# Cross-attention over a long context on one core: two batches a step, each with all its keys on 64 TensorE columns

## The chip, the core and the metric

One core of a Trainium2 chip runs the whole program in one launch. The metric is the device time of an execution in microseconds (us). The kernel before took 1009.78, 1009.5 and 1008.39 us in three runs; their median, 1009.5 us, is what the change is compared with.

## The reference, cut to what matters

The block is layer norm, self-attention, cross-attention, a two-layer feed-forward part, a gated recurrent layer and a mixture of eight experts. The change is in the cross-attention. It has 16 batches of 64 query rows and 1601 context rows, all 512 wide:

```python
def cross_attn(x, context, Wq, Wk, Wv):
    Q = x @ Wq
    K, V = (context @ Wk, context @ Wv)
    energy = jnp.einsum('bqd,bkd->bqk', Q, K)
    Sk = energy.shape[-1]
    lengths = jnp.sum(energy[:, 0] != 0, axis=-1)
    kidx = jnp.arange(Sk)
    pad = kidx[None, None, :] >= lengths[:, None, None]
    energy = jnp.where(pad, NEG_INF, energy)
    score = jax.nn.softmax(energy / np.sqrt(DK), axis=-1)
    return jnp.einsum('bqk,bkd->bqd', score, V)
z = cross_attn(x, context, Wq2, Wk2, Wv2)
x = layer_norm(x + z, ln2_g, ln2_b)
z = jax.nn.relu(x @ fc1_w + fc1_b)
z = z @ fc2_w + fc2_b
```

The kernel folds the weights: the queries are multiplied by Wq times the transposed Wk, scores are taken against the raw context, and Wv is applied to the attention's output. So the context is wanted in two layouts, both in HBM and both loaded: `ctxT`, with the 512 features on the partitions (for the scores), and `ctx`, with keys on the partitions (for the weighted sums, called values below).

## The kernel before, in words

Every engine has its own program, written out by hand in program order, and the programs meet in semaphores. TensorE does the matmuls (weight loads are a row of their own in the profile, PEld), VectorE (DVE) and ScalarE (ACT) evacuate PSUM, GpSimd (POOL) makes the low parts of weights, and SyncE (SP) issues all loads of this stage, in order, each behind the waits that stand ahead of it.

Cross-attention runs in 17 rounds, one batch a round, and each round finishes the batch before. TensorE's array is used in two halves of 64 columns: the two halves take the same 64 queries and different keys of one batch, the wide one 833 keys and the narrow one 768, and `WIDE` alternates which half is wide. A TensorE round n is:

- `scores(n)` (L621): two pieces of up to 512 columns, four chunks of features, two halves.
- `transpose_probabilities(n-1)` (L631): 7 transposes, the last of 65 columns.
- `transpose_output(n-2)` (L663): 4 transposes of the attention's output.
- a filling, by the tables `LATE` (part of the queries of later batches, L598) or `VALUE` (`value_rows(i)`, the product with Wv of token tile i, 12 matmuls of split fp32 at L486).
- `exchange(n)` (L670, L673): maxima and sums of the two halves are swapped between them and the keys counted.
- `values(n-1)` (L650, 12 matmuls, and L654, the 65 last keys, on one half alone).

VectorE counts the non-zero scores (`count_keys`, L1469), builds the mask and takes the row maximum (`shift`, L1490 and L1495), combines the halves' factors (`normaliser`), adds the two halves' outputs (`output_sum`, L1525), makes the low part of the output (`output_low`, L1533) and, after a `value_rows(i)`, adds it to x and normalises (`second_norm(i)`: L1538, L1315, L1317, L1320, POOL's L1935, L1332, L1336). ScalarE does the exponential (L1102) and scaled copies. `decay_start`, `decay_term` and `decay_end` are a chain of small VectorE operations for the recurrent layer (`lac`), spread over the rounds.

`VALUE` puts tiles 0 to 5 into rounds 9 to 14 and tile 6 into round 16, ahead of the last values. Tile 7 follows the loop. There TensorE does the transposes `t2` of the normalised rows (L493, in groups of four tiles' quarters), the last output's transposes, `value_rows(7)`, and then the first half of fc1 (L486 on `f1u`).

The context is held in two whole-batch buffers for each layout (`cT`, `nat`). SP loads `ctxT` of batch n+1 once the scores of n-1 are done with the buffer (`e_done`), and `ctx` of batch n once the values of n-2 are (`pv_done`):

```python
def load_columns(n):
    load(cT[n % 2], a["ctxT"][n].rearrange("p (c k) -> p c k", c=DC), ct_in[n % 2])
```

At the start, both layouts of two batches are loaded before any score is taken. The weight units of fc1 (`f1u`) are loaded after the scores of the last batch; ScalarE makes their high part and POOL their low part (L1958).

## Time and profile before

| | |
|---|---|
| three runs | 1008.39 to 1009.78 us, median 1009.5 |
| profiled execution | 1006.8 us, of which the span is 1005.1 |
| TensorE busy (PE) | 985.9 us, 98% of the span |
| VectorE, ScalarE, GpSimd busy | 614.8, 393.7, 215.9 us |
| cross-attention, first scores to first fc1 matmul | 112.55 to 370.46 us of the span |
| chain that ended last | PE 85%, DVE 7%, DMA 6% |
| loaded from HBM | 190 MB, mostly context |

The profile is of one execution, 2.7 us shorter than the median of the runs. Times in rows are microseconds from the start of the span. A group of matmuls in a timeline is one row with a count; the bracket behind a row says how long its engine had been idle and what released it. A KB of the profile's DMA issues is 1024 bytes.

### The profile page before, as it was taken

The numbers are of one execution on the slowest core, as the hardware profiler recorded it, in microseconds if no ns is written. First come the engines' busy times: TensorE is split into PE (matmuls) and PEld (weight loads), VectorE is DVE, ScalarE is ACT, GpSimd is POOL, SyncE is SP. The second block draws the span as 40 slices with busy tenths as digits, with TensorE's granted clock in tenths as the row PEclk, the third lists the DMA queues.
The fourth block names the chain that finished last, engine by engine and source line by source line (L and its number), as shares of the span: only waits on it lengthen the run. The fifth ranks groups of instructions, "written<-read, shape, count | busy, mean of one in ns | idle before, by whom it ended". The sixth has DMA issues, their size and how long they took to land.

```text
span 1005.1 us, 14411 instructions
## 1 busy us (share of the span) xinstructions
PE 985.9 (98%) x5412; PEld 777.0 (77%) x5412; DVE 614.8 (61%) x1142; ACT 393.7 (39%) x631; POOL 215.9 (21%) x202
## 2 busy tenths in 40 slices
PE   7999999999999999999999999899999999999998
PEld 4886444445454468878888887899999999999997
DVE  6368443344655565896466668577665666656666
ACT  3332211222111143355667542444544444445441
POOL 2053400002000036454422124720000000000051
PEclk9999999999999999999999999999999999999999
DMA  9809599999999922033311100885764756645543
GB/s 295 317 1 381 241 361 417 409 414 397 415 396 408 388 94 74 1 92 108 110 42 38 32 1 7 277 283 156 217 188 151 206 159 196 189 155 183 152 150 133
DMA packets 45959, 206.91 MB, mean 206 GB/s; under 512 B 5760, under 2 KB 16256, under 8 KB 41680
## 3 DMA queue, kind: packets, MB, share of 16 engines
q1 hardware_dynamic: 40256, 187.95, 52.6%
q0 software_dynamic: 5648, 18.22, 5.4%
q8 instruction: 34, 0.56, 0.2%
q14 instruction: 21, 0.17, 0.0%
HBM read 190.04 MB, written 16.12 MB: 205 GB/s over the span
## 4 chain that ended last, share of the span: by engine, by line
PE 85%; DVE 7%; DMA 6%; issue 1%; ACT 0%; SPq 0%; POOL 0%; DVEq 0%; ACTq 0%
PE ps L486 59%; PE ps L621 7%; PE ps L650 7%; DMA big<-in_ctxT 3%; DMA big<-in_ctx 2%; DVE stats L1315 2%; PE ps L480 2%; PE ps L598 1%; PE ps L951 1%; PE ps L856 1%; PE ps L978 1%; PE ps L654 1%; PE ps L631 1%; PE ps L493 1%; DVE hr L1324 1%; PE ps L532 1%
## 5 line engine op out<-in xcount | busy, mean ns | idle before, releaser
L486 PE MATMUL ps<-x,w 128*128 128x320 f32 x1536 | 235.6, 309 | 0.0
L486 PEld LDWEIGHTS ps<-x,w 128*128 128x128 f32 x1536 | 228.0, 188 | 0.4
L1839 DVE TENSOR_TENSOR w<-big,w 128x1536 fp32r<-128x1536 f32 x64 | 112.1, 1753 | 78.3 <-ACT w L1249 78.3
L486 PE MATMUL ps<-hsplit,w 128*128 128x320 f32 x672 | 107.7, 309 | 0.0
L1249 ACT CAST w<-big 128x1536 fp32r<-128x1536 f32 x64 | 94.2, 1475 | 29.2 <-PE ps L486 27.0
L486 PEld LDWEIGHTS ps<-hsplit,w 128*128 128x128 f32 x672 | 100.8, 188 | 0.1
L486 PE MATMUL ps<-xcT,u 128*128 128x512 f32 x432 | 98.2, 389 | 0.0
L621 PE MATMUL ps<-big 128*64 128x512 f32 (+2 forms) x512 | 95.9, 500 | 0.7 <-DVE s_stat L1495 0.6
L486 PEld LDWEIGHTS ps<-xcT,u 128*128 128x128 f32 x432 | 81.0, 188 | 17.0 <-DVE xcT L1627 0.2
L650 PE MATMUL ps<-big 128*64 128x512 f32 x384 | 86.4, 597 | 1.7 <-DMA big<-in_ctx 1.5
L621 PEld LDWEIGHTS ps<-big 128*64 128x64 f32 x512 | 44.2, 136 | 51.0 <-issue 39.1
L1271 ACT CAST hsplit<-big 128x320 fp32r<-128x320 f32 x64 | 29.4, 460 | 137.9 <-DVE big L1869 137.9
L1958 POOL TENSOR_TENSOR u<-big,u 128x512 fp32r<-128x512 f32 (+1 forms) x40 | 59.4, 1493 | 103.5 <-ACT u L1088 103.5
L2043 POOL DMA_DIRECT2D ys<-big x28 | 16.8, 603 | 276.3 <-DVE big L1861 275.3
L1935 POOL TENSOR_TENSOR rstd<-veps,consts 128x1 f32<-128x1 f32 x48 | 34.0, 709 | 182.2 <-DVE veps L1320 181.9
L486 PE MATMUL ps<-hT,u 128*128 128x512 f32 x288 | 66.0, 390 | 0.8 <-DVE big L1616 0.7
L486 PEld LDWEIGHTS ps<-hT,u 128*128 128x128 f32 x288 | 53.9, 188 | 12.6 <-issue 0.9
L650 PEld LDWEIGHTS ps<-big 128*64 128x64 f32 x384 | 26.1, 137 | 46.8 <-issue 44.8
L1474 DVE COPY big<-ps 128x512 f32<-128x512 f32 x16 | 11.1, 691 | 77.3 <-PE ps L631 77.3
L1020 ACT COPY big<-ps 128x512 f32<-128x512 f32 (+1 forms) x48 | 24.5, 543 | 75.1 <-PE ps L486 47.3
L1873 DVE TENSOR_TENSOR hsplit<-big,hsplit 128x320 fp32r<-128x320 f32 (+1 forms) x72 | 32.0, 454 | 33.7 <-ACT hsplit L1271 33.7
L1102 ACT ACTIVATE big<-big,s_work 128x833 f32<-128x833 f32 x16 | 15.8, 991 | 59.8 <-DVE s_work L1498 59.8
(336 smaller groups left out, 1544.6 us busy)
## 6 DMA issues: line engine op xcount, KB each, us to landing
big<-in_ctxT SPq DMA_DIRECT2D x16, 3202.0 KB, 19.3
big<-in_ctx SPq DMA_DIRECT2D x16, 3072.0 KB
big<-in_w_units SPq DMA_DIRECT2D x64, 768.0 KB, 4.4
big<-in_dense_units SPq DMA_DIRECT2D x41, 256.0 KB, 2.7
xs<-big POOLq DMA_DIRECT2D x1, 5120.0 KB, 17.4
big<-in_gate_units SPq DMA_DIRECT2D x12, 384.0 KB, 3.0
hr<-xs SPq DMA_DIRECT2D x28, 160.0 KB, 5.8
ys<-big POOLq DMA_DIRECT2D x28, 160.0 KB, 5.6
```

The lines of the kernel that those rows point to most:

```text
L480: mm = nc.tensor.matmul(bank(*g)[:, 0:cols], lhsT, rhs, start=(k == 0), stop=(k == len(pairs) - 1))
L486: mm = nc.tensor.matmul(dst, lhs[x], rhs[w], start=start and x + w == 0, stop=stop and x == 1)
L621: mm = nc.tensor.matmul(ps[half * S:half * S + S, 2 + piece, 0:w], qT[:, d, n * S:(n + 1) * S], cT[n % 2][:, d, col:col + w], start=(d == ...
L650: mm = nc.tensor.matmul(ps[half * S:half * S + S, 6, :], pts[:, t, half * S:half * S + S], nat[j][:, narrow * KH + t, :], start=(t == 0), ...
L1020: signals_evacuated(nc.scalar.copy(dst, src_bank), *g)
L1249: nc.scalar.copy(wsplit[f % RING][0][:], wraw[f % RING]).then_inc(w_high, 1)
L1271: nc.scalar.copy(hsplit[f % 2][:, 0:SLOTS], hid[f % 2]).then_inc(hid_high, 1)
L1315: V.bn_stats(stats[:, i, :], src).then_inc(ln_stats, 1)
L1839: V.tensor_tensor(wsplit[f % RING][1][:], wraw[f % RING], wsplit[f % RING][0][:].bitcast(F32), ALU.subtract).then_inc(w_low, 1)
L1873: V.tensor_tensor(h[:, to:to + hi - lo], hid[f % 2][:, lo:hi], h[:, lo:hi].bitcast(F32), ALU.subtract).then_inc(hid_low, 1)
L1935: G.tensor_tensor(rstd[:, i:i + 1], veps[:, i:i + 1], consts[:, 0:1], ALU.pow).then_inc(ln_rstd[L], 1)
L1958: G.tensor_tensor(low[:, 0:w], unit_raw(u)[:, 0:w], high[:, 0:w].bitcast(F32), ALU.subtract).then_inc(u_low, 1)
```

## The change

A step p now takes two batches, 2p and 2p+1, each with all 1601 keys on its own 64 columns of TensorE. There are nine steps instead of 17 rounds.

- `scores(p)` (new L634) has three pieces of 512 keys and one of 65, four chunks, two halves, in four PSUM banks. `transpose_probabilities(p)` (L656) has 12 transposes into three banks; the thirteenth, of the last 65 keys (L674), stands beside the count's matmul (L677). The swap of maxima and sums, the factors and `output_sum` are gone. `values(p)` has 24 matmuls (L691) and 2 for the last keys (L698). `transpose_output` comes once a pair, and `output_low(p)` (L1522) reads PSUM and writes 512 columns.
- VectorE's passes over the scores are 1601 columns wide instead of 833, once a pair.
- `VALUE` gives a step up to two tiles, one ahead of the values and one behind; step 8 has tile 6 behind the last values. `late_queries(p)` comes whole in steps 0 to 3.
- The context goes through five ring slots of two buffers, 8 KB a partition each (1 MB a load). Columns and rows share the slots, which are filled in the order of use: three slots of columns of pair p+1, three of rows of pair p. A slot is loaded again when its piece has been used (`piece_used`). The last 65 columns and rows have two small buffers each. `ctxT` is packed in pieces in HBM. fc1's units are loaded after piece 45 of 48 was used.

```diff
-PIECES = ((0, 512, 512), (512, KA - 512, KH * P - 512))
-WIDE = [n // 2 % 2 for n in range(B)]
-LATE = {1: (0, 0, 2), 2: (0, 2, 4), 3: (1, 0, 2), 4: (1, 2, 4), 5: (2, 0, 4), 6: (3, 0, 2), 7: (3, 2, 4)}
-VALUE = {9: 0, 10: 1, 11: 2, 12: 3, 13: 4, 14: 5, 16: 6}
+PAIRS = B // 2
+PIECES = KT // 4
+RINGS = 5
+VALUE = {5: (0, 1), 6: (2, 3), 7: (4, 5), 8: (None, 6)}
...
-            def load_context(n):
-                j = n % 2
-                load(nat[j][:, 0:KT, :], a["ctx"][n, 0:KT * P, :].rearrange("(p k) d -> p k d", k=KT), nat_in[j])
-                load(nat[j][0:TAIL, KT, :], a["ctx"][n, KT * P:SK, :], nat_in[j])
-
-            def load_columns(n):
-                load(cT[n % 2], a["ctxT"][n].rearrange("p (c k) -> p c k", c=DC), ct_in[n % 2])
+            def load_pieces(rows, p):
+                for piece in range(PIECES):
+                    g = loads[0]
+                    loads[0] += 1
...
+                    if g >= RINGS:
+                        sp.wait_ge(piece_used, g - RINGS + 1)
+                    for half in range(2):
+                        n, to = 2 * p + half, context_at[g % RINGS][half]
+                        if rows:
+                            keys = a["ctx"][n, 0:KT * P, :].rearrange("(p k) d -> p k d", k=KT)
+                            load(to, keys[:, 4 * piece:4 * piece + 4, :], context_in[g % RINGS])
+                        else:
+                            load(to, a["ctxT"][n * PIECES + piece].rearrange("p (c k) -> p c k", c=DC), context_in[g % RINGS])
...
             load_columns(0)
-            load_context(0)
-
-            for i in range(NT):
-                wait_filled(sp, "z", i)
-            load_columns(1)
-            load_context(1)
-            sp.wait_ge(e_done, 1)
-            load_columns(2)
-            for n in range(2, B):
-                if n + 1 < B:
-                    sp.wait_ge(e_done, n)
-                    load_columns(n + 1)
-                if n == 8:
+            for p in range(1, PAIRS):
+                load_columns(p)
+                if p == 5:
                     sp.wait_ge(late_q, DC)
                     for k in range(DC):
                         load(z2_raw[k], a["dense_units"][k], u_in[k])
-                sp.wait_ge(pv_done, n - 1)
-                load_context(n)
-            sp.wait_ge(e_done, B)
+                load_rows_of(p - 1)
+            load_rows_of(PAIRS - 1)
+            sp.wait_ge(piece_used, 2 * PAIRS * PIECES - PIECES)
...
+            def scores(p):
...
+                for piece in range(PIECES + 1):
...
                     for d in range(DC):
...
-                        for half in (WIDE[n], 1 - WIDE[n]):
-                            narrow = half != WIDE[n]
-                            col, w = narrow * KA + lo, widths[narrow]
+                        for half in range(2):
+                            n, w = 2 * p + half, 512 if piece < PIECES else TAIL
                             mm = nc.tensor.matmul(ps[half * S:half * S + S, 2 + piece, 0:w], qT[:, d, n * S:(n + 1) * S],
-                                                  cT[n % 2][:, d, col:col + w], start=(d == 0), stop=(d == DC - 1))
-                mm.then_inc(e_done, 1)
+                                                  columns_in[half][:, d, :], start=(d == 0), stop=(d == DC - 1))
+                    mm.then_inc(piece_used if piece < PIECES else e_done, 1)
...
+            for p in range(PAIRS + 1):
+                if p < PAIRS:
+                    scores(p)
+                if p == 0:
+                    late_transposes(4, NT - 1)
+                    tail_and_count(0)
+                    late_transposes(NT - 1, NT)
+                    late_queries(0)
+                    continue
+                transpose_probabilities(p - 1)
+                if p >= 2:
+                    transpose_output(p - 2)
+                tail_and_count(p)
+                if p < PAIRS // 2:
+                    late_queries(p)
+                ahead, behind = VALUE.get(p, (None, None))
+                if ahead is not None:
+                    value_rows(ahead, 3 * p)
+                values(p - 1)
+                if behind is not None:
+                    value_rows(behind, 3 * p)
...
             split_transposes("t2", 0)
             split_transposes("t2", 1)
-            transpose_output(B - 1)
+            transpose_output(PAIRS - 1)
             split_transposes("t2", 2)
-            pe.wait_ge(o_evac, 2 * B - 1)
+            pe.wait_ge(o_evac, PAIRS)
             split_transposes("t2", 3)
-            value_rows(NT - 1)
+            value_rows(NT - 1, 3 * PAIRS)
...
+            for p in range(PAIRS + 1):
+                if p < PAIRS:
+                    count_keys(p)
+                tail_and_count(p)
+                if p < PAIRS:
+                    shift(p)
+                if p:
+                    normaliser(p - 1)
+                if p >= 2:
+                    output_low(p - 2)
+                for i in VALUE.get(p, ()):
+                    if i is not None:
+                        second_norm(i)
...
+                if p == 8:
+                    decay_end()
+            output_low(PAIRS - 1)
```


How the instructions stand on three engines, where it matters:

SP's loads at the start, before (`in_ctxT` is the context with features on the partitions, `in_ctx` that with keys):

```order
L368 DMA big<-in_ctxT 128x6404
L368 DMA big<-in_ctx 128x6144
L368 DMA big<-in_ctx 65x512
L368 DMA big<-in_ctxT 128x6404
L368 DMA big<-in_ctx 128x6144
L368 DMA big<-in_ctx 65x512
L368 DMA big<-in_ctxT 128x6404 x2
```

and with the change:

```order
L363 DMA big<-in_ctxT 128x2048 x6
L363 DMA big<-in_ctx_tails 128x520
L363 DMA big<-in_ctxT 128x2048 x6
L363 DMA big<-in_ctx_tails 128x520
L363 DMA big<-in_ctx 128x2048 x6
L363 DMA big<-in_ctx 65x512 x2
```

One batch's columns and rows were two large loads and a small one; now three slots of columns, six loads of 2048 elements a partition, come for a pair, with one small load for the last columns.

TensorE's last round of the loop and what follows it, before (`z2u` are parts of Wv, `oT` the transposed output):

```order
L631 MATMUL ps<-ident,big 128x128 x6
L631 MATMUL ps<-ident,big 65x128
L663 MATMUL ps<-ident,big 128x128 x4
L486 MATMUL ps<-z2u0high,oT_high 128x512
...
L486 MATMUL ps<-z2u3high,oT_low_74 128x512
L670 MATMUL ps<-s_stat,swap 128x2
L650 MATMUL ps<-big 64x512 x12
L654 MATMUL ps<-big 64x512
L493 MATMUL ps<-ident,hr 128x128 x8
L663 MATMUL ps<-ident,big 128x128 x4
L493 MATMUL ps<-ident,hr 128x128 x8
L486 MATMUL ps<-z2u0high,oT_high 128x512
```

and with the change, from the last scores (its L493 is the line that was L486):

```order
L634 MATMUL ps<-big 64x512 x24
L634 MATMUL ps<-big 64x65 x8
L656 MATMUL ps<-ident,big 128x128 x12
L667 MATMUL ps<-ident,big 128x128 x4
L674 MATMUL ps<-ident,big 65x128
L677 MATMUL ps<-s_cnt,first_rows 128x1
L493 MATMUL ps<-z2u0high,oT_high 128x512
...
L493 MATMUL ps<-z2u3high,oT_low_74 128x512
L691 MATMUL ps<-big 64x512 x24
L698 MATMUL ps<-big 64x512 x2
L493 MATMUL ps<-z2u0high,oT_high 128x512
```

`value_rows(6)` stood ahead of the last values and the `t2` transposes right behind them; now value rows 5 (the first `z2u` rows) stand ahead of the last values, and value rows 6 between those and the transposes.

VectorE's end of the stage, before (the normaliser's last operation has gone ahead; `hr` is the second norm of tile 6, `oT_low_75` the last output's low part, `hT` the first operand of fc1):

```order
L1533 TENSOR_TENSOR oT_low_75<-oh_rk,oT_high 128x4x64
L1538 TENSOR_TENSOR hr<-hr,ps 128x512
L1315 BN_STATS stats<-hr 128x6
L1317 BN_AGGR mv<-stats 128x2
L1320 TENSOR_SCALAR veps<-mv 128x1
L1332 SCALAR_TENSOR_TENSOR hr<-hr,mv,lnw 128x512
L1336 SCALAR_TENSOR_TENSOR hr<-hr,rstd,lnw 128x512
L1525 TENSOR_REDUCE oh_rk<-ps 128x256
L1533 TENSOR_TENSOR oT_low_75<-oh_rk,oT_high 128x4x64
L1580 TENSOR_TENSOR hT_115<-ps,hT_114 128x4x128 x4
```

and with the change:

```order
L1527 TENSOR_TENSOR hr<-hr,ps 128x512
L1335 BN_STATS stats<-hr 128x6
L1337 BN_AGGR mv<-stats 128x2
L1340 TENSOR_SCALAR veps<-mv 128x1
L1352 SCALAR_TENSOR_TENSOR hr<-hr,mv,lnw 128x512
L1356 SCALAR_TENSOR_TENSOR hr<-hr,rstd,lnw 128x512
L1469 TENSOR_TENSOR lac<-lac 128x6
L1470 TENSOR_SCALAR lac<-fbase 128x6
L1472 SCALAR_TENSOR_TENSOR lac<-lac 128x6
L1473 SCALAR_TENSOR_TENSOR lac<-lac 128x6
L1522 TENSOR_TENSOR oT_low_75<-ps,oT_high 128x512
L1566 TENSOR_TENSOR hT_115<-ps,hT_114 128x4x128 x4
```

The last output's low part was behind the second norm of tile 6 too; now four operations of `decay_end` (`lac`) stand between, and the second norm waits for value rows that come after the last values.

## Rows read from the trace of the kernel before

**Rows 1.** Page, DMA issues: tensors, queue, count, KB each, us to landing.

```profile
big<-in_ctxT SPq DMA_DIRECT2D x16, 3202.0 KB, 19.3
big<-in_ctx SPq DMA_DIRECT2D x16, 3072.0 KB
```

**Rows 2.** Windows: stretch, us, busy PE, PEld, DVE, ACT, POOL (count), PEclk, DMA, GB/s.

```profile
76.00:140.00 64.00, 60.96 (x262) 32.97 (x262) 38.56 (x77) 14.44 (x38) 19.36 (x16) 1.00 0.79 317
80.00:108.00 28.00, 26.74 (x97) 16.65 (x96) 26.96 (x46) 5.68 (x11) 15.39 (x14) 1.00 1.01 423
140.00:180.00 40.00, 40.00 (x215) 19.43 (x213) 17.60 (x58) 9.15 (x23) 0.00 (x0) 1.00 1.01 415
140.00:340.00 200.00, 199.77 (x1045) 99.14 (x1043) 101.11 (x309) 40.73 (x100) 8.51 (x10) 1.00 1.01 407
256.60:338.20 81.60, 81.50 (x426) 42.62 (x425) 46.39 (x138) 14.00 (x35) 2.74 (x5) 1.00 1.00 402
631.00:636.00 5.00, 5.00 (x41) 4.99 (x41) 1.55 (x11) 1.75 (x4) 2.99 (x4) 1.00 0.99 415
643.00:644.00 1.00, 1.00 (x5) 1.00 (x5) 1.00 (x1) 0.02 (x1) 0.69 (x2) 0.50 0.26 102
```

**Rows 3.** Timeline, TensorE's weight loads: start, us, engine, line, operation, [idle before <-releaser].

```profile
256.60 0.20 PEld L621 LDWEIGHTS ps<-big 128*64 128x64 f32 x4 [0.78 <-DMA big<-in_ctxT]
...
338.22 0.20 PEld L621 LDWEIGHTS ps<-big 128*64 128x64 f32 x4 [0.74 <-DMA big<-in_ctxT]
...
346.90 0.20 PEld L650 LDWEIGHTS ps<-big 128*64 128x64 f32 x4 [1.75 <-DMA big<-in_ctx]
```

**Rows 4.** Chain of waits, 280 to 306: start, us, what (one round).

```profile
289.50 5.81 PE ps L621 x30
...
296.22 0.44 PE ps L663 x4
296.66 2.75 PE ps L486 x12
...
299.74 5.30 PE ps L650 x24
305.04 0.85 PE ps L654 x2
```

**Rows 5.** Timeline, first scores, 112 to 123.

```profile
112.55 5.81 PE L621 MATMUL ps<-big 128*64 128x512 f32 x32
...
118.42 1.02 DVE L1469 TENSOR_SCALAR_CACHE_REDUCE big<-ps 128x833 f32<-128x833 f32 x1 [4.87 <-PE ps L621]
...
122.32 1.08 PE L621 MATMUL ps<-big 128*64 128x512 f32 x4 [0.62 <-DVE s_stat L1495]
```

**Rows 6.** Timeline, end of cross-attention, 340 to 371.

```profile
340.93 0.16 DVE L1449 TENSOR_TENSOR lac<-lac 128x6 f32<-128x6 f32 x1
...
360.22 0.68 DVE L1538 TENSOR_TENSOR hr<-hr,ps 128x512 f32<-128x512 f32 x1
363.36 1.02 PE L654 MATMUL ps<-big 65*64 65x512 f32 x2
363.48 0.75 DVE L1336 SCALAR_TENSOR_TENSOR hr<-hr,rstd,lnw 128x512 f32<-128x512 f32 x1
...
367.57 0.50 PE L486 MATMUL ps<-z2u0high,oT_high 128*128 128x512 f32 x1 [0.24 <-DVE oT_low L1533]
...
370.46 0.86 PE L486 MATMUL ps<-hT,f1u 128*128 128x512 f32 x3
```

**Rows 7.** Timeline, last normalisation before the fc1 activations, 370 to 377.

```profile
370.66 0.69 DVE L1538 TENSOR_TENSOR hr<-hr,ps 128x512 f32<-128x512 f32 x1 [0.76 <-PE ps L486]
...
373.08 3.00 POOL L1958 TENSOR_TENSOR f2u<-big,f2u 128x512 fp32r<-128x512 f32 x2
...
374.96 1.67 DVE L1336 SCALAR_TENSOR_TENSOR hr<-hr,rstd,lnw 128x512 f32<-128x512 f32 x1
```

**Rows 8.** Timeline, TensorE after a long wait in the last stage.

```profile
642.45 0.54 PE L856 MATMUL ps<-pick,row4high 128*128 128x320 f32 x1 [2.84 <-DVE pick L1764]
```

More of the change, by code:

```diff
@@ L610, in scores @@
+            used = [0]
+            def scores(p):
+                if p:
+                    pe.wait_ge(shifted, p)
+                else:
                     for c in range(DC - 1):
                         wait_evacuated(pe, "q", c)
-                for piece, (lo, *widths) in enumerate(PIECES):
-                    if piece and n % 2 == 0:
-                        pe.wait_ge(pad_cleared, n // 2 + 1)
+                if p == PAIRS // 2:
+                    pe.wait_ge(late_q_out, DC)
+                for piece in range(PIECES + 1):
+                    if piece < PIECES:
+                        g = used[0]
+                        used[0] += 1
+                        pe.wait_ge(context_in[g % RINGS], 32 * (g // RINGS + 1))
+                        columns_in = context_at[g % RINGS]
+                    else:
+                        pe.wait_ge(column_tail_in[p % 2], 16 * (p // 2 + 1))
+                        columns_in = column_tails[p % 2]
@@ L615, in scores @@
                     for d in range(DC):
-                        if n == 0 and d == DC - 1:
+                        if p == 0 and piece == 0 and d == DC - 1:
                             wait_evacuated(pe, "q", DC - 1)
-                        for half in (WIDE[n], 1 - WIDE[n]):
-                            narrow = half != WIDE[n]
-                            col, w = narrow * KA + lo, widths[narrow]
+                        for half in range(2):
+                            n, w = 2 * p + half, 512 if piece < PIECES else TAIL
@@ L637, in values @@
-            def values(n, lo, hi):
-                j = n % 2
-                if lo == 0:
-                    pe.wait_ge(nat_in[j], 32 * (n // 2 + 1))
-                    pe.wait_ge(pt_evac[0], n + 1)
-                    if n:
-                        pe.wait_ge(o_copied, n)
-                else:
-                    pe.wait_ge(pt_evac[1], 2 * n + 2)
-                for t in range(lo, hi):
-                    for half in (WIDE[n], 1 - WIDE[n]):
-                        narrow = half != WIDE[n]
-                        mm = nc.tensor.matmul(ps[half * S:half * S + S, 6, :], pts[:, t, half * S:half * S + S],
-                                              nat[j][:, narrow * KH + t, :], start=(t == 0), stop=(narrow and t == KH - 1))
-                if hi == KH:
-                    w = slice(WIDE[n] * S, WIDE[n] * S + S)
-                    mm = nc.tensor.matmul(ps[w, 6, :], pts[0:TAIL, KH, w], nat[j][0:TAIL, KT, :], start=False, stop=True)
-                    mm.then_inc(pv_done, 1)
@@ L1134, in _ @@
                     nc.scalar.copy(fbias[:], lnw[:, 6, :]).then_inc(fb_high, 1)
+                if p == 4:
+                    for u in range(DC):
+                        unit_high(u)
             def transposed_high(name, i):
@@ L1153, in _ @@
             transposed_high("t2", 1)
-            output_out(B - 1)
+            output_out(PAIRS - 1)
             unit_high(5)
@@ L1541, in second_norm @@
                 norm_gain(2, i, hr[:, i, :], lnw[:, 3, :])
-            for n in range(B + 1):
-                if n:
-                    probabilities_out(n - 1)
-                if n < B:
-                    count_keys(n)
-                if n >= 2:
-                    output_sum(n - 2)
-                exchanged(n)
-                if n < B:
-                    shift(n)
-                if n:
-                    normaliser(n - 1)
-                if n >= 2:
-                    output_low(n - 2)
-                if n in VALUE:
-                    second_norm(VALUE[n])
-                if n == 6:
-                    decay_start()
-                if 7 <= n < 7 + ATANH_TERMS - 2:
-                    decay_term(ATANH_TERMS + 5 - n)
-                if n == 5 + ATANH_TERMS:
-                    decay_end()
-                if n == 4:
+            for p in range(PAIRS + 1):
+                if p < PAIRS:
+                    count_keys(p)
+                tail_and_count(p)
+                if p < PAIRS:
+                    shift(p)
+                if p:
+                    normaliser(p - 1)
+                if p >= 2:
+                    output_low(p - 2)
+                for i in VALUE.get(p, ()):
+                    if i is not None:
+                        second_norm(i)
+                if p == 2:
                     dve.wait_ge(fb_high, 1)
@@ L1569, in _ @@
                     V.tensor_tensor(fbias[S:P, :], lnw[S:P, 6, :], fbias[S:P, :].bitcast(F32), ALU.subtract).then_inc(fb_low, 1)
-            output_sum(B - 1)
-            output_low(B - 1)
+                if p == 3:
+                    decay_start()
+                if 4 <= p < 8:
+                    for k in range(ATANH_TERMS - 2 - 2 * (p - 4), max(ATANH_TERMS - 4 - 2 * (p - 4), 0), -1):
+                        decay_term(k)
+                if p == 8:
+                    decay_end()
+            output_low(PAIRS - 1)
             dve.wait_ge(lnw_in, 16)
```

360 lines of the change are left out of this document (161 added, 199 removed).

## The prediction, made before the changed kernel was run

> **What bounds the kernel now.** I read first the page's DMA issues, then windows over cross-attention, then TensorE's waits in it, then its end. A batch brings 3202 KB of `ctxT`, 3072 KB of `ctx` and 130 KB of last rows (65 rows of 2 KB, from the code), 6404 KB or 6.56 MB [rows 1]. From 140 to 340 us the DMA engines are busy all the time at 407 GB/s, and TensorE is busy all the time too [rows 2]. The stage is bound by both, and the timeline of weight loads says how closely: at 256.60 and, five batches later, at 338.22 the scores wait 0.78 and 0.74 us for their `ctxT` [rows 3]; I counted four more such waits between. Five batches in 81.62 us are 16.32 us a batch and 402 GB/s, as the window of that stretch shows. So the load stream sets the pace, and TensorE's round, with value rows, fills it: 5.81 us of scores, 0.44 of output transposes, 2.75 of value rows, 5.30 and 0.85 of values, and some smaller pieces [rows 4].
>
> At the end the stream runs out before TensorE does. The rows of batch 14 come at 346.90 [rows 3]; those of batch 15, 3202 KB, are the last of the context and come 8.2 us later at 402 GB/s, at 355.1. The last values end at 363.36 + 1.02 = 364.4, and fc1 starts at 370.46, 6.1 us behind them [rows 6]. From there on the program is unchanged, so I forecast the start of fc1 and carry its shift to the end.
>
> **The change part by part.**
>
> *TensorE's work in the loop.* A pair's values are 24 + 2 matmuls in both halves: twice 5.30, and one 0.85 for the last keys in place of two. A 512-column piece of scores is 5.81 x 512/833 = 3.6 us; three and the 65 last columns make 11.2 in place of 11.6. Output transposes fall from 0.88 to 0.44 a pair, and the swaps go [rows 4]. That is about 2 us a pair, 16 in all. But a pair with two value rows then takes about 30 us, while its 13.1 MB at 402 GB/s take 32.6. TensorE waits for pieces instead. I cost this saving at nothing; the load stream covers it, and the bytes are the same.
>
> *VectorE and ScalarE.* A pass of 833 columns takes 1.02 us [rows 5]; 1601 columns are 1.96 by proportion, once a pair instead of twice. Busy 101 of 200 us [rows 2], VectorE has room; at the start alone it is waited for (next step).
>
> *The start of the stream.* Before, two batches, 13.1 MB, are loaded ahead, and by 140 us 64 x 0.317 = 20.3 MB have come [rows 2]. The ring holds 5 slots of 2.10 MB and 0.27 MB of last columns, 10.75 MB. At 423 GB/s [rows 2] it is full by about 103, and the stream stands until the first piece is used: scores start at 112.55 [rows 5], plus 3.6 for a piece is 116.1. Before, 20.3 - 13.1 = 7.2 MB came between the issue behind the first scores (118.4) and 140, 17.7 us of stream at 407, so 3.9 us were lost to latency and to the wait for the second scores. With pieces freed every 3.6 us I take 2.4 us of it: from 118.5, 21.5 us at the 415 GB/s of the first window behind 140 [rows 2] are 8.9 MB, in all 19.65. That is 0.65 MB or 1.5 us behind. Bounds: 0.5 (no more than 1.4 us lost) and 3.0 (all 3.9). The second scores wait for the first's VectorE passes: before from 118.4 to 122.32 [rows 5], now 2.5 us more and scores that end 5 us later; they start near 130. TensorE has late transposes and queries there, and the ring is full, so only those 1.5 us count.
>
> *The pace of the stream.* Loads become 1 MB with 8 KB a partition instead of 3.2 MB with 25 KB. No row shows this size. The nearest is the expert weights, 768 KB loads with 6 KB a partition back to back: 415 GB/s [rows 2]. The stream itself went at 415 early and 402 late, 407 on the mean. I take no change, with 1% to either side, 2.2 us on some 217 us of stream. A rule of the Trainium skill speaks against the change here: "DMA: Bandwidth & Descriptors", section "Bandwidth", gives 1 MB transfers 78% of the peak and 16 MB ones 97%. Scaled so from 407 the stream would fall to some 330 GB/s, an estimate from that page, and the sum would be about +55 us. By that rule the 768 KB loads could not have gone at 415 [rows 2]; the trace disagrees, and I give it 2 in 100, within rival C.
>
> *The end of the values.* The last piece lands at 355.1 + 1.5 = 356.6. It has four of twelve key tiles of each batch: 5.30 x 4/6 = 3.5 us, and the last keys 0.85 [rows 4]: 361.0, 3.4 us earlier than before. Here the change gains, since before TensorE still had two batches' leftovers when the stream ended.
>
> *From the last values to fc1.* This is new work in series. Before, `value_rows(6)` came ahead of the last values, and `second_norm(6)` ran beside them, from 360.22 to 363.48 + 0.75 [rows 6]. Now TensorE starts `value_rows(6)` behind them, 2.75 us. The second norm follows: 4.0 us alone [rows 6], 6.0 us from 370.66 to 374.96 + 1.67 where two POOL passes stand beside it [rows 7]. Behind it in VectorE's order come `decay_end`, four operations of 0.16 [rows 6], and only then the last `output_low`, about 0.68 for 512 columns. TensorE's next transposes wait for that: 0.44, then `value_rows(7)` 2.75 and about 0.25 to start each [rows 4, 6]. The last output's own transposes, ready by then, are off this path. The sum is 2.75 + 4.0 + 0.65 + 0.68 + 0.44 + 2.75 + 0.5 = 11.8 us, or 13.8 with POOL's passes beside the norm. POOL's passes come here one by one with ScalarE's casts between, so I take the middle, 12.8.
>
> *The clock.* In that stretch TensorE has 2 us of transposes and an idle time of about 5 us. In the last stage, after an idle time of 2.84 us, its granted clock falls to 0.50, which is 1.2 of 2.4 GHz [rows 2, 8]. The transposes and value rows behind the wait, 3.2 us, cost between nothing and 3.2 us more at that clock; half of it, 1.6, is taken, since the clock came back within a few us in that stage.
>
> **Sum.** 361.0 + 12.8 + 1.6 = 375.4 for the start of fc1, against 370.46: +4.9 us. The profiled execution's 1006.8 us becomes 1011.7; it stands 2.7 below the median of the runs, so the median of 1009.5 becomes **1014.4**. The bounds together are 1.0 to 1.6 us each for start, tail and clock: its own range is 1010.8 to 1018.5.
>
> **The rivals.** A difference below 0.2%, 2 us, is about what a measurement here can't tell from no change.
>
> *A, faster: the stream runs faster in pieces.* The first stretch went at 423 GB/s [rows 2], and 415 is seen for 6 KB a partition. TensorE's 30 us a pair leave room to 437. Each 1% is worth 2.2 us, and since the forecast is +4.9, it takes 3.2%, 420 GB/s, to be faster by 2 us; at 425 it is -9.6, so 1004.8. Against it: the stream's share was full before too, so there is no idle time between loads to win.
>
> *B, about the same: the new tail costs less.* No POOL pass beside the norm (-1.0), no fall of the clock (-1.6), and 0.5% of pace (-1.1) leave +1.2, 1010.7. For it: clock and contention are only seen elsewhere.
>
> *C, much slower: TensorE's clock falls inside the loop.* TensorE now waits in small portions: 3.6 us of piece, then up to 1.8 until the next lands. At half clock a pair's 30 us would become up to 60, more than the 32.6 of its loads; every 2.6 us spent at half clock beyond that slack goes to the end. If a third of the last three pairs ran so, 3 x (40 - 32.6) = 22 us. In this trace waits of 0.7 to 1.75 us left the clock at 1.00 [rows 2, 3], and only the 2.84 did not. The Trainium skill, "TensorE: Matmul & The Clock Gate", section "HAM oscillation — how this bites in real kernels", has kernels where each wait for a slice makes the next start at the low clock; by these rows it would not here, outside the tail. So 1036. A slower pace belongs here too: 395 GB/s, 3% below the mean of 407, is +6.6 on the forecast, 1021.
>
> That the change doesn't do what it says I give nothing: the order of the instructions shows pieces, pairs and tables moved as described.
>
> **How the numbers follow.** Forecast 0.50 (slower), A 0.15 (faster), B 0.20 (the same), C 0.15 (slower). So faster 0.15, same 0.20, slower 0.65. The range 1006.5 to 1020 holds the forecast's own, B, and the near part of A and C; it leaves out about one in ten at either end.
>
> **What the next profile would show.** Right: DMA share full from about 119 to 357 but for gaps near 105 to 118, 402 to 415 GB/s; TensorE waiting for `ctxT` and `ctx` pieces in most of the loop at clock 1.00; the last values ending near 361; then value rows 6, a wait of some 5 us for the last `output_low`, clock 0.5 behind it, fc1 at about 375. Wrong: a stream above 420 GB/s or below 398 in the same stretch; granted clock below 1 inside the loop; fc1 before 372.5 or after 379.

## The result, and the profile after

The changed kernel took 1020.1 us (median of four runs, 1019.28 to 1021.72) against 1009.0 of the kernel before in the same comparison: a ratio of 1.0112, 95% interval 1.0096 to 1.0128, so 11.1 us slower. The direction was forecast, the size was not: +4.9 had been worked out, and 1020.1 lies just above the range's end of 1020. The profiled execution took 1020.73 us with a span of 1019.0, 13.9 more than the span before. fc1 starts at 384.44, 13.98 us later than the 370.46 of [rows 6]. (The two profiled executions lie 2.8 us further apart than the medians: the one before is 2.2 us below 1009.0, the one after 0.6 above 1020.1.) So the whole loss is ahead of fc1, and the two parts of it can be read apart at the end of the last values: 368.1 (forecast 361.0) and 16.3 us from there to fc1 (forecast 14.4).

The page of the changed kernel: the span, TensorE, the chain by engine, and the two large kinds of loads.

```profile
span 1019.0 us, 14013 instructions
PE 977.5 (96%) x5324; PEld 755.8 (74%) x5324; DVE 568.9 (56%) x933; ACT 385.7 (38%) x575; POOL 216.4 (21%) x202
PE 80%; DMA 11%; DVE 8%; issue 1%; SPq 0%; ACT 0%; POOL 0%; DVEq 0%; ACTq 0%
big<-in_ctxT SPq DMA_DIRECT2D x48, 1024.0 KB, 17.2
big<-in_ctx SPq DMA_DIRECT2D x48, 1024.0 KB, 18.1
```

TensorE is 8.4 us less busy and the span is longer: the saved work became waits for loads. Windows over the stage (columns as in [rows 2]):

```profile
76.00:140.00 64.00, 61.36 (x254) 31.16 (x255) 35.27 (x57) 13.39 (x33) 19.36 (x16) 1.00 0.73 295
132.00:134.00 2.00, 2.00 (x12) 0.67 (x10) 0.00 (x0) 1.36 (x2) 0.00 (x0) 1.00 0.79 328
134.00:136.00 2.00, 2.00 (x12) 0.72 (x10) 0.00 (x0) 0.00 (x0) 0.00 (x0) 1.00 0.39 57
136.00:138.00 2.00, 2.00 (x12) 0.61 (x10) 0.00 (x0) 0.00 (x0) 0.00 (x0) 1.00 0.75 283
140.00:340.00 200.00, 183.62 (x943) 76.89 (x941) 58.59 (x134) 34.06 (x54) 7.17 (x8) 0.99 1.01 401
206.00:208.00 2.00, 2.00 (x12) 0.61 (x10) 0.00 (x0) 0.44 (x2) 0.00 (x0) 1.00 1.09 293
208.00:210.00 2.00, 2.00 (x12) 0.71 (x10) 0.00 (x0) 0.00 (x0) 0.00 (x0) 1.00 1.04 267
212.00:214.00 2.00, 2.00 (x12) 0.62 (x10) 0.00 (x0) 0.00 (x0) 0.00 (x0) 1.00 1.02 426
244.00:246.00 2.00, 2.00 (x8) 0.73 (x6) 0.00 (x0) 0.00 (x0) 0.00 (x0) 0.50 0.99 410
340.00:356.00 16.00, 14.86 (x75) 7.05 (x73) 4.39 (x10) 2.96 (x7) 0.92 (x2) 1.00 1.01 367
380.00:382.00 2.00, 2.00 (x7) 1.66 (x6) 1.85 (x3) 1.42 (x3) 0.24 (x1) 0.50 0.14 53
```

By 140 us 64 x 0.295 = 18.9 MB have come, against 20.3 before [rows 2]. The stream stands twice: once until the first piece is used, and again at 132 to 138, when the ring is full once more and the first columns of pair 1 are not yet used. From 140 to 340 it moves 401 GB/s with the DMA engines always busy. That mean hides two speeds: about 420 in most windows of 2 us (their median is 418), and dips of some 4 us, one a pair, here 293 and 267, where the two small loads of last rows of a pair (65 partitions, 2 KB each) pass; run 5 leaves them out, and the dips go. In the dips the DMA share is 1.04 to 1.09: the engines don't stand, they move less. The kernel before has such dips too, down to 298 in a window of 2 us. TensorE's waits for pieces, its last values, POOL's passes, TensorE's long wait at the end and its first matmul of fc1, from the timeline:

```profile
220.70 0.20 PEld L634 LDWEIGHTS ps<-big 128*64 128x64 f32 x4 [2.10 <-DMA big<-in_ctxT]
...
242.34 5.35 PE L691 MATMUL ps<-big 128*64 128x512 f32 x16 [2.42 <-DMA big<-in_ctx]
...
363.59 0.20 PEld L691 LDWEIGHTS ps<-big 128*64 128x64 f32 x4 [1.72 <-DMA big<-in_ctx]
...
367.08 1.03 PE L698 MATMUL ps<-big 65*64 65x512 f32 x4
...
373.55 4.60 POOL L1944 TENSOR_TENSOR f1u<-big,f1u 128x512 fp32r<-128x512 f32 x3
...
379.43 1.11 PE L500 MATMUL ps<-ident,hr 128*128 128x128 f32 x4 [6.58 <-DVE oT_low L1522]
...
384.44 5.84 PE L493 MATMUL ps<-hT,f1u 128*128 128x512 f32 x25
```

Its first wait for a piece is at 215.83 (0.32 us), the first long one at 220.70. From the first on it waits for 16 of 27 pieces, and the last piece comes at 363.59, where 356.6 was forecast. Behind it, the chain of waits:

```profile
363.59 3.65 PE ps L691 x16
367.25 0.86 PE ps L698 x4
368.11 3.01 PE ps L493 x12
...
371.14 0.70 DVE hr L1527
...
373.62 1.76 DVE hr L1352
...
375.40 1.63 DVE hr L1356
377.03 1.15 DVE lac L1469
...
378.68 0.70 DVE oT_low L1522
...
379.43 1.11 PE ps L500 x4
380.54 5.66 PE ps L493 x19
```

This is the series that was forecast: value rows 6, the second norm of tile 6, the decay chain, the last low part, the transposes, value rows 7. The norm takes 5.9 us, with POOL's passes beside its two long ones (1.76 and 1.63 against 0.75 in [rows 6]), and the first small operation 1.15.

### The profile page after: what moved, and what is told of

The parts are those of the page before. It is cut to its first block, busy times and chain, and to the rows that moved or that the text cites. A ratio compares the mean times of both kernels' runs of the same rounds, so it can differ in the third digit from the quotient of the medians.

```text
span 1019.0 us, 14013 instructions
## 1 busy us (share of the span) xinstructions
PE 977.5 (96%) x5324; PEld 755.8 (74%) x5324; DVE 568.9 (56%) x933; ACT 385.7 (38%) x575; POOL 216.4 (21%) x202
## 4 chain that ended last, share of the span: by engine, by line
PE 80%; DMA 11%; DVE 8%; issue 1%; SPq 0%; ACT 0%; POOL 0%; DVEq 0%; ACTq 0%
PE ps L493 58%; DMA big<-in_ctxT 8%; PE ps L634 6%; PE ps L691 4%; DMA big<-in_ctx 2%; DVE stats L1335 2%; PE ps L487 1%; PE ps L606 1%; PE ps L974 1%; PE ps L879 1%; PE ps L1001 1%; PE ps L656 1%; PE ps L500 1%; DVE hr L1352 1%; DVE hr L1344 1%; PE ps L539 1%
## 5 line engine op out<-in xcount | busy, mean ns | idle before, releaser
L493 PE MATMUL ps<-x,w 128*128 128x320 f32 x1536 | 235.6, 309 | 0.0
L493 PEld LDWEIGHTS ps<-x,w 128*128 128x128 f32 x1536 | 228.0, 188 | 0.4
L493 PE MATMUL ps<-hsplit,w 128*128 128x320 f32 x672 | 107.7, 309 | 0.0
L493 PEld LDWEIGHTS ps<-hsplit,w 128*128 128x128 f32 x672 | 100.8, 188 | 0.1
L493 PE MATMUL ps<-xcT,u 128*128 128x512 f32 x432 | 98.2, 389 | 0.0
L634 PE MATMUL ps<-big 128*64 128x512 f32 (+1 forms) x512 | 89.4, 502 | 8.6 <-DMA big<-in_ctxT 8.6
L691 PE MATMUL ps<-big 128*64 128x512 f32 x384 | 87.4, 606 | 9.4 <-DMA big<-in_ctx 9.4
L493 PEld LDWEIGHTS ps<-xcT,u 128*128 128x128 f32 x432 | 81.0, 188 | 17.0 <-DVE xcT L1613 0.2
L1484 DVE TENSOR_SCALAR_CACHE_REDUCE big<-ps 128x1601 f32<-128x1601 f32 x8 | 14.6, 1825 | 135.1 <-PE ps L634 135.1
L634 PEld LDWEIGHTS ps<-big 128*64 128x64 f32 x512 | 31.8, 137 | 70.5 <-issue 55.6
L691 PEld LDWEIGHTS ps<-big 128*64 128x64 f32 x384 | 26.6, 139 | 66.7 <-issue 51.1
L493 PE MATMUL ps<-hT,u 128*128 128x512 f32 x288 | 66.1, 390 | 0.8 <-DVE big L1602 0.8
L493 PEld LDWEIGHTS ps<-hT,u 128*128 128x128 f32 x288 | 53.9, 188 | 12.7 <-issue 1.0
L1116 ACT COPY big<-ps 128x512 f32<-128x512 f32 x24 | 12.6, 594 | 78.7 <-PE ps L656 78.7
```

The costliest lines, as they stand in the source:

```text
L493: mm = nc.tensor.matmul(dst, lhs[x], rhs[w], start=start and x + w == 0, stop=stop and x == 1)
L634: mm = nc.tensor.matmul(ps[half * S:half * S + S, 2 + piece, 0:w], qT[:, d, n * S:(n + 1) * S], columns_in[half][:, d, :], start=(d == 0), ...
L691: mm = nc.tensor.matmul(ps[half * S:half * S + S, 6, :], pts[:, t, half * S:half * S + S], context_at[g % RINGS][half][:, t % 4, :], start ...
```

## The experiments

All ratios are to the kernel before, measured beside the run.

**1. Value rows 6 ahead of the last values again.**

```diff
-VALUE = {5: (0, 1), 6: (2, 3), 7: (4, 5), 8: (None, 6)}
+VALUE = {5: (0, 1), 6: (2, 3), 7: (4, 5), 8: (6, None)}
```

> Value rows of tile 6 stand ahead of the last values again; all else as in the change. Theory (the new series of work behind the last values costs 10 us, 16.3 against 6.1 before): from the last values to fc1 it falls to 6 to 7 us. The last values then start behind the value rows, which wait for the low part of output 6 (358.5 in the changed kernel), so they end near 372.8 instead of 368.1, and fc1 starts near 379 instead of 384.4: 5 us faster than the change, 1015. Rival (the delay is all in the stream, and the tail costs only what any order would): no change, 1020.

Measured: 1018.37 us, ratio 1.0083 (1.0054 to 1.0112). That is 1.7 us below the change, and the two intervals overlap. The timeline says why it won no more:

```profile
361.20 0.50 PE L493 MATMUL ps<-z2u0high,oT_high 128*128 128x512 f32 x1 [3.54 <-DVE oT_low L1522]
...
376.10 1.03 PE L698 MATMUL ps<-big 65*64 65x512 f32 x4
...
384.01 11.04 PE L493 MATMUL ps<-hT,f1u 128*128 128x512 f32 x48
```

From the last values, 377.1, to fc1 it is 6.9 us, so the length of the end is explained. But TensorE waited 3.5 us for the low part of output 6, which VectorE makes behind the norm of tile 5, with all values queued behind that wait.

**2. The last low part ahead of the norm on VectorE.**

```diff
+                if p == 8:
+                    output_low(PAIRS - 1)
                 for i in VALUE.get(p, ()):
...
                     decay_end()
-            output_low(PAIRS - 1)
```

> VectorE makes the last output's low part ahead of the second norm of tile 6 and of the four operations of the decay chain. Theory (fc1 does not need that norm; it waits only because of VectorE's order): value rows 7 then wait only for the first addition of the norm, fc1 starts near 377.6 instead of 384.4, 6 to 7 us faster, 1013.5. TensorE's idle time shrinks from 6.6 us to about 2, and the clock stays at 1.00. Rival (the norm is needed, or the clock falls all the same): less than 3 us faster.

Measured: 1023.45 us, ratio 1.014 (1.0113 to 1.0166). The theory misses:

```profile
384.46 13.70 PE L493 MATMUL ps<-hT,f1u 128*128 128x512 f32 x48 [7.46 <-DVE hT L1567]
```

fc1 starts no earlier; it now waits 7.46 us for the low part of its own operand `hT`, which VectorE makes behind the same norm and the same decay chain. fc1 does not need the norm, but it needs VectorE, and the norm came late whichever of the two stands first. Behind that longer idle time fc1 itself runs at a lower clock: from 384 to 420 the mean granted clock is 0.92, with the change 1.00.

**3. Tail rows as 64 and 1.** In `load_rows_of`, with the wait counting 64:

```diff
-                    load(row_tails[p % 2][half][0:TAIL, :], a["ctx"][2 * p + half, KT * P:SK, :], row_tail_in[p % 2])
+                    load(row_tails[p % 2][half][0:S, :], a["ctx"][2 * p + half, KT * P:KT * P + S, :], row_tail_in[p % 2])
+                    load(row_tails[p % 2][half][S:TAIL, :], a["ctx"][2 * p + half, KT * P + S:SK, :], row_tail_in[p % 2])
```

> The 65 last context rows of a batch come as a load of 64 partitions and a load of one, instead of one load of 65. Theory (the load on 65 partitions, a number that doesn't divide over 16 DMA engines, slows the large loads beside it, as the dips to 210 to 330 GB/s at 206 to 211 and 239 to 244 us say): the dips go, the stream between 140 and 340 us rises from 401 towards 415 GB/s, the last rows land 5 to 8 us earlier, and the time falls by as much, to 1012 to 1015. Rival (the dips come from what the bytes are or where they lie, 2 KB rows, not from the number of partitions): the same dips, 1020.

Measured: 1023.85 us, ratio 1.0136 (1.0099 to 1.0174). The dips are as deep as before:

```profile
140.00:340.00 200.00, 183.70 (x932) 77.01 (x929) 56.11 (x128) 32.78 (x53) 7.17 (x8) 0.97 1.02 398
206.00:208.00 2.00, 2.00 (x12) 0.61 (x10) 0.00 (x0) 0.43 (x2) 0.00 (x0) 1.00 1.10 281
208.00:210.00 2.00, 2.00 (x12) 0.72 (x10) 0.00 (x0) 0.00 (x0) 0.00 (x0) 1.00 1.03 263
```

The dips stay, so 65 as a number that doesn't divide over 16 is not shown to be the reason; but a load of one row came with the 64, and run 10, with 80 rows, is the cleaner test. The granted clock in the loop is a little lower here (0.97 against 0.99), which may be why the time is above the change's.

**4. Four ring slots.** `RINGS = 4` for 5.

> Four ring slots instead of five. Theory (what counts is the amount loaded ahead of the first scores, because the stream never stops afterwards): 2.1 MB less ahead, 5.0 us of stream at 415 GB/s, 1025. Rival 1 (the amount ahead is hidden, the pace of the stream alone counts): no change, 1020. Rival 2 (the ring is too short in the loop too, so that loads wait for slots): over 10 us slower, with the DMA share in the loop below 0.95.

Measured: 1025.21 us, ratio 1.0158 (1.0128 to 1.0187), 5.1 above the change.

```profile
76.00:140.00 64.00, 61.38 (x256) 31.29 (x256) 35.27 (x57) 13.41 (x33) 19.37 (x16) 1.00 0.64 261
140.00:340.00 200.00, 180.36 (x927) 75.00 (x924) 54.70 (x125) 32.78 (x53) 7.18 (x8) 0.99 1.01 403
```

By 140 us 16.7 MB have come, 2.2 less than with five slots; behind that the stream is as fast. What isn't loaded ahead comes later, about byte for byte.

**5. Tail rows for two pairs only.**

```diff
-                for half in range(2):
+                for half in range(2) if p < 2 else ():
```

> The last 65 context rows are loaded for pairs 0 and 1 only; later pairs use those again, so this leaves 12 of the 16 small loads of 130 KB out (1.6 MB, 4 us of stream by their bytes). Theory (each of these loads costs the large loads beside it more than its bytes, as the dips say: 0.25 to 0.35 MB or 0.7 us): the last rows land 8 us earlier, at 355 instead of 363.6, the dips are gone after pair 1, and the time is 1012. Rival (they cost their bytes): 4 us, 1016.

Pairs 2 to 7 take the last rows of other batches here, so the kernel leaves out part of the work. Measured: 1008.34 us, ratio 0.9999 (0.9989 to 1.0008), 11.8 below the change.

```profile
140.00:340.00 200.00, 191.62 (x991) 80.51 (x988) 61.27 (x139) 35.20 (x56) 7.72 (x9) 1.00 1.01 415
206.00:208.00 2.00, 2.00 (x12) 0.71 (x10) 0.00 (x0) 0.26 (x2) 0.00 (x0) 1.00 1.01 414
208.00:210.00 2.00, 2.00 (x12) 0.57 (x9) 0.00 (x0) 0.00 (x0) 0.00 (x0) 1.00 0.99 414
```

The dips behind 200 are gone, so they are those loads, and they cost nearly three times the 4 us of their bytes.

**6. The kernel before with 8 KB loads.** The large loads of both layouts are split in three:

```diff
-                load(cT[n % 2], a["ctxT"][n].rearrange("p (c k) -> p c k", c=DC), ct_in[n % 2])
+                flat = cT[n % 2].rearrange("p c k -> p (c k)")
+                for lo, hi in ((0, 2048), (2048, 4096), (4096, DC * SK)):
+                    load(flat[:, lo:hi], a["ctxT"][n][:, lo:hi], ct_in[n % 2])
```

> The kernel before, with each large load split into three of 8 KB a partition (8 and 9 KB for the columns), the same buffers and waits. If small loads carry less (a reason for the late landing in the changed kernel), the stream of 140 to 340 us falls from 407 towards 400 GB/s, and the time rises by 3 us or more, to 1012.5. Theory (the size of the load costs nothing; between dips the changed kernel's stream runs at 419 to 422 GB/s): no change, 1009.5, within 2 us.

Measured: 1012.11 us, ratio 1.0042 (1.0025 to 1.0059). The first expectation holds, and the theory is out: smaller loads carry less here.

```profile
140.00:340.00 200.00, 194.93 (x1016) 96.24 (x1014) 94.19 (x295) 39.28 (x96) 7.70 (x9) 1.00 1.01 397
```

**7. Value rows 6 ahead of the last piece.** They stand inside the last `values`, and VectorE makes output 6's low part ahead of the scaling of tile 5:

```diff
+                    if t == 7 and p == PAIRS - 1:
+                        value_rows(6, 3 * PAIRS)
...
                     if i is not None:
-                        second_norm(i)
+                        second_add(i)
+                        if i != 5:
+                            second_scale(i)
+                if p == 8:
+                    second_scale(5)
+                    decay_end()
+                    second_norm(6)
```

> The changed kernel with value rows 6 between the second and third piece of the last values, and on VectorE the low part of output 6 ahead of the scaling of tile 5's norm, the decay chain ahead of tile 6's norm. Theory (value rows 6 behind the last values is the cost; at their first place, in the run with them ahead of all values, they waited 3.5 us for that low part): no wait for it, the last values end near 370.1, 2 us later, fc1 starts 6.9 us behind them, near 377, against 384.4: 1013. Rival (the wait moves elsewhere on VectorE, as it did in the run with the last low part first): less than 3 us faster.

Measured: 1013.57 us, ratio 1.0037 (1.0023 to 1.0052), 6.5 below the change.

```profile
369.97 1.03 PE L700 MATMUL ps<-big 65*64 65x512 f32 x4
...
374.55 0.66 PE L500 MATMUL ps<-ident,hr 128*128 128x128 f32 x4 [1.60 <-DVE oT_low L1524]
...
377.83 1.55 PE L493 MATMUL ps<-hT,f1u 128*128 128x512 f32 x6
```

fc1 starts 6.8 us behind the last values, and of the 6.6 us of idle time 1.6 are left. So the order of the end cost 6.5 us.

**8. Tail rows on 128 partitions.** 63 rows of no use come with them:

```diff
+                    n = 2 * p + half
+                    if n < B - 1:
+                        start = n * SK + KT * P
+                        load(row_tails[p % 2][half], a["ctx"].rearrange("b s d -> (b s) d")[start:start + P, :], row_tail_in[p % 2])
```

> The 65 last rows of a batch are loaded with the 63 rows behind them in memory (not used), 128 partitions of 2 KB, except for the last batch. 1.9 MB more in all, 4.5 us of stream. Theory (the small loads slow the others because they crowd on 65 partitions): the dips go, 0.35 to 0.7 us less each, 15 times, minus 4.5 us: 1015 to 1020. Rival (they cost by bytes and number of rows): the dips are longer, 1024.5 or more.

Measured: 1013.24 us, ratio 1.0047 (1.003 to 1.0064), 6.9 below the change with 1.9 MB more to load.

```profile
140.00:340.00 200.00, 187.44 (x971) 78.63 (x969) 61.29 (x139) 34.50 (x55) 7.71 (x9) 1.00 1.02 417
206.00:208.00 2.00, 2.00 (x12) 0.72 (x10) 0.29 (x3) 1.00 (x2) 0.00 (x0) 1.00 1.02 392
208.00:210.00 2.00, 2.00 (x12) 0.69 (x10) 0.00 (x0) 0.00 (x0) 0.00 (x0) 1.00 1.02 411
```

**9. Both mends**, of runs 7 and 8.

> Both mends together: value rows 6 before the last piece, and tail rows loaded on 128 partitions. Theory (stream and end of the stage are separate losses and add): 1020.1 - 6.5 - 6.9 = 1006.7, 2 us below the kernel before. Rival (with the stream faster, TensorE ends last and the moved value rows cost it more than they save): 1010 or more.

Measured: 1005.67 us, ratio 0.9968 (0.9956 to 0.998). The losses are separate and add, within 1 us; mended, the change is 3 us faster than the kernel before as it stood (runs 11 and 12 mend that kernel too).

**10. As run 9 with 80 rows.** The width P of run 8's load is 80.

> As the run before, but 80 rows (five on each of 16 engines if they are dealt out so) in place of 128. 1.5 MB less to load for 15 batches. Theory (it is the uneven split of 65 rows over 16 engines that slows): as good as with 128 or up to 3.5 us better, 1003 to 1007. Rival (it is the crowding on some of the 128 partitions): dips as with 65, 1013.

Measured: 1012.57 us, ratio 1.004 (1.0025 to 1.0055). The theory is out: the stream is back at its old pace, though 80 is five times 16.

```profile
140.00:340.00 200.00, 182.98 (x941) 76.89 (x939) 57.61 (x133) 33.07 (x54) 7.17 (x8) 0.99 1.02 400
208.00:210.00 2.00, 2.00 (x12) 0.72 (x10) 0.00 (x0) 0.00 (x0) 0.00 (x0) 1.00 1.07 288
```

**11. The kernel before with tail rows on 128 partitions**, loaded as in run 8 into `nat`.

> The kernel before with the tail rows on 128 partitions, its large loads as they were. Its stream at 407 GB/s would rise to 415 or more by bytes, of which 1.9 MB are of no use. TensorE is busy 199.77 of 200 us, so nothing is won: 1008 to 1010. If TensorE's 0.8 us of waits a round were the bound, up to 4 us faster, 1005.

Measured: 1002.92 us, ratio 0.9942 (0.9929 to 0.9956), the fastest of all and faster than either expectation. TensorE's weight loads waited 6.5 us for context loads in the kernel before (six times for `ctxT`, 4.7 us, and once for `ctx`, 1.8); here they wait for none. Busy 199.77 of 200 us had hidden what those waits cost.

```profile
140.00:340.00 200.00, 199.87 (x1064) 100.23 (x1060) 102.63 (x314) 40.76 (x100) 8.51 (x10) 1.00 1.01 426
```

**12. The kernel before with both edits**, 8 KB loads and 128 rows.

> The kernel before with 8 KB loads and the tail rows on 128 partitions. With 8 KB loads and 65 rows the stream was 397 GB/s and the time 1012. Theory (8 KB loads are slow only beside loads on 65 partitions): the stream is 412 to 418 GB/s and the time 1008 to 1010. Rival (8 KB loads are slower by themselves): 1012.

Measured: 1004.87 us, ratio 0.9962 (0.9949 to 0.9975), faster than either expectation; by the pace, the theory is nearer.

```profile
140.00:340.00 200.00, 199.52 (x1054) 104.20 (x1050) 102.21 (x311) 40.77 (x100) 8.51 (x10) 1.00 1.01 419
```

With the kernel before, the pace of 140 to 340 us makes a square: 25 KB loads 407 with 65 rows and 426 with 128; 8 KB loads 397 and 419. The 65 rows cost 19 to 22 GB/s, the smaller loads 7 to 10. (About a fiftieth of the stream with 128 rows is rows that nobody reads; without them the 65 rows still cost some 11 to 14.) Each corner is one profiled execution.

Like for like the change still loses: with the tail rows mended on both sides, run 9 takes 1005.67 us and run 11 takes 1002.92. In run 9 fc1 starts at 369.44, in run 11 at 366.39. Against run 12, which has the 8 KB loads too, 0.8 us are left, and the intervals overlap.

**13. The same 65 rows on partitions 32 to 96.** The last transpose takes the 97 last columns, so that the probabilities lie there too, and the matmul of the last keys is split:

```diff
-                    load(row_tails[p % 2][half][0:TAIL, :], ...
+                    load(row_tails[p % 2][half][32:32 + TAIL, :], ...
...
+                    for lo, hi in ((32, 64), (64, 32 + TAIL)):
+                        mm = nc.tensor.matmul(ps[half * S:half * S + S, 6, :], pts[lo:hi, KT, half * S:half * S + S],
+                                              row_tails[p % 2][half][lo:hi, :], start=False, stop=(lo == 64))
```

> The changed kernel with the same 65 tail rows a batch in one load, put on partitions 32 to 96 instead of 0 to 64; the last transpose is of 97 columns, and the matmul of the last keys is split into rows 32 to 63 and 64 to 96. Theory (partitions 0 to 63 share half of the ports; 32 to 95 spread over all): the stream of 140 to 340 us is 415 to 420 GB/s, as with 128 rows, with 1.9 MB less to load, so 1 to 4 us below that run's 1013.2: 1009 to 1012. Rival (any load of 65 partitions is slow, since 65 doesn't divide over 16 engines): 401 GB/s and 1020.

Measured: 1034.24 us, ratio 1.0252 (1.0236 to 1.0267). The theory misses, and the time is no verdict on it, since TensorE became the bound. Windows, then the timeline's split matmuls:

```profile
140.00:340.00 200.00, 199.67 (x934) 79.28 (x931) 52.75 (x121) 30.92 (x50) 7.17 (x8) 0.96 1.01 400
206.00:208.00 2.00, 2.00 (x27) 1.83 (x23) 1.63 (x1) 1.06 (x3) 0.00 (x0) 1.00 1.08 353
208.00:210.00 2.00, 1.99 (x9) 1.20 (x8) 1.49 (x5) 0.99 (x3) 0.00 (x0) 1.00 1.02 278
```

```profile
374.35 4.40 PE L699 MATMUL ps<-big 32*64 32x512 f32 x8
```

What can be read is in the windows: the dips are there with the rows on other partitions.

**14. Run 13 with run 7's order.**

> As the run before, with value rows 6 before the last piece. If TensorE, which did not wait for the last pieces with 128 rows, is now the bound at the end, it equals that run, 1005.7; if the stream still counts, 1002 to 1005. Either way it is below the kernel before. By the rival of the run before (no port, but the count of partitions) 1013.

Measured: 1027.62 us, ratio 1.018 (1.0156 to 1.0204), missing both expectations for the same reason: with the split matmuls TensorE is busy 199.68 us of 140 to 340.

## Why the prediction was right and wrong

**What bounds the kernel** was right. The stream sets the pace, TensorE's saved work became waits, and what came late in the stream came late at fc1.

**"The pace of the stream ... I take no change, with 1% to either side"** is the step that failed most. 401 GB/s in place of 407 over 200 us are 1.2 MB, 3.0 us, where the margin allowed 2.2. What the runs show in its place is the size of the loads: the kernel before, with its loads split to 8 KB and all else kept, falls from 407 to 397 (run 6), and with 128 tail rows from 426 to 419 (run 12). Larger loads in the changed kernel were not tried. I had set the 8 KB loads beside 768 KB loads at 415 that ran alone.

The small loads of 65 rows are a second thing that I had not looked for, but they don't explain the drop: they are in the 407 that I started from, and cost 19 GB/s there and 16 with the change (417 in run 8). They explain why the pace had more room than I saw. My argument against rival A, that a full DMA share leaves nothing to win, is wrong: in the dips the share is full, and the pace is not. Rival A itself did not come: 8 KB pieces without the 65-row loads run at 415 to 419, under its 420, and run 8 is still 0.5% slower than the kernel before.

The rule I had weighed there, of the Trainium skill's "DMA: Bandwidth & Descriptors", section "Bandwidth", has the right sign and the wrong size: 426 to 419 GB/s from 3 MB to 1 MB loads, not a fifth. The table there is of transfers issued from GpSimd; these come from SP, several in flight.

**The start** was sized at 1.5 us (bounds 0.5 and 3.0). Measured are 20.3 - 18.9 = 1.4 MB, 3.4 us, beyond the bound. I counted the wait for the first piece and missed the second standstill at 132 to 138: slots freed by pair 0 fill again before the second scores begin. Run 4 shows that bytes ahead are worth their time.

Start and pace are 3.4 + 3.0, where 1.5 was forecast: 4.9 of the 7.0 us by which the last piece is late. The other 2 us fall behind 340, where the forecast took 402 GB/s and the window to 356 shows 367 and that from 356 to 364 shows 264. One more dip lies there; what else slows the last loads was not tried.

**The end of the values** was right in form: 363.59 + 3.65 + 0.86 is the last piece plus 4.5 us. But the forecast had a gain here, the last values 3.4 us earlier than before; they end 3.7 us later (368.1 against 364.4).

**From the last values to fc1** the series had every member right, at 16.3 against 14.4 us. The norm had POOL beside its two long passes (5.9, where I took the middle of 4.0 and 6.0), and the decay chain took 1.6 for 0.65, since its first operation stood beside POOL too. Rival B, a cheap end, is out. The end is 10.2 us longer than the 6.1 before, where the forecast had 8.3 with the clock; run 7 wins back 6.5 of it by the order alone.

**The clock** was sized nearly right, at 1.6 us: behind 6.58 us of idle time the granted clock is 0.50 (1.2 of 2.4 GHz), value rows 7 took 380.2 to 384.4, 4.2 us in place of 2.8, and the four transposes ahead of them 1.11 in place of 0.66. Rival C's mechanism came once in the loop, behind 2.42 us of idle time at 242.34, where the granted clock fell to 0.50 and a piece took 5.35 in place of 3.65; behind 2.32 us at 277.92 the granted clock stayed at 1.00. The stream covers that one: the next piece of columns is still waited for, 0.23 us at 248.78. So of the signs of being wrong that were named, two came: a clock below 1 inside the loop, and fc1 after 379.

**The sum.** fc1 came 9.0 us after the forecast's 375.4: 3.0 of pace, 1.9 of start, some 2 behind 340, 0.1 in the last values, 1.9 in the end. By the medians the miss is 5.7 us (1020.1 against 1014.4): the forecast put the profiled execution before 2.7 below its median, and the one after lies 0.6 above its own. The forecast owed its sign to the end of the stage alone; what stands before it had been forecast as a gain and was a loss.

## What to carry to other kernels

Before a load stream is cut into other sizes, look at it in windows of 2 us: a mean rate hides small loads that slow everything beside them, though the DMA share stays full, and mending those can be worth more than the change (here 5.8 us for the kernel before, by loading 63 rows that nobody reads). When a mend helps both kernels, give it to both before they are compared: here that turns a gain of 3 us into a loss of 2.7. When steps are merged into fewer, larger ones, list what now stands behind the last transfer on each engine, small operations and norms included, and move whatever does not need it ahead of it. A ring that holds less than what was loaded ahead before gave that back here, about byte for byte (run 4).

## What the runs showed of the hardware

Loads of 2 KB rows on 64, 65 or 80 partitions pull the stream down to 263 to 353 GB/s in the windows shown; on 128 partitions, with more bytes, they don't (392 to 411). Short rows alone are not the reason: the last columns, 260 KB in rows of 2 KB on 128 partitions, pass in the changed kernel between 190 and 194, and its windows there show 404 and 432. The Trainium skill, "SBUF — State Buffer", section "Door 1: The DMA port swizzle", says that bandwidth depends on how many of 16 ports the partitions reach, and its table puts partitions 0 to 63 on eight of them. Dips with 64 rows and none with 128 fit that rule; 80 rows, by the table on twelve ports, dip as deep (288 shown), and the run with partitions 32 to 96, which by the rule reach all sixteen, does not fit. What it is in these loads stays open. It is not the division by 16 (80 rows dip too); counts between 80 and 128, and another place of the rows in HBM, were not tried.

Splitting the matmul of the last keys, over 65 partitions, into two over 32 and 33 at bases of 32 and 64 was dear: the four parts of a pair took 4.06 to 4.40 us where two whole ones took 0.86 (chain) to 1.03. The first four, at 158.28, took their 4.06 us at a granted clock of 1.00, so it is not the clock. Later in that run the granted clock did fall to 0.50 (286 to 292) with TensorE shown busy throughout; its mean over 140 to 340 is 0.96. Why was not tried.
